# Moving four small copies from ScalarE to VectorE, and a read of PSUM behind a sum, in a fused attention and expert kernel

## The reference

```python
q, k, v = (proj(Wq, bq), proj(Wk, bk), proj(Wv, bv))      # tanh(states @ W + bias), per head
alpha = jnp.einsum('bhqd,bhkd->bhqk', q, k) / jnp.sqrt(jnp.float32(d))
alpha = jnp.where(causal, alpha, jnp.finfo(jnp.float32).min)
alpha = jax.nn.softmax(alpha, axis=-1)
ctx = jnp.einsum('bhqk,bhkd->bhqd', alpha, v)
ctx = ctx.transpose(0, 2, 1, 3).reshape(b, s, h * d)
return jnp.tanh(ctx @ Wo + bo)
...
x = x + _layernorm(_L0_attn_ref(_layernorm(x, axis=-1), ...), axis=-1)
x = x + _layernorm(_L0_ffn_ref(_layernorm(x, axis=-1), ...), axis=-1)
```

## Time and profile before

| | |
|---|---|
| device time of the profiled execution | 1604.17 us |
| its span, first to last instruction | 1602.3 us |
| median of three executions | 1609.84 us |
| TensorE matmul busy | 1522.1 us (95%) |
| VectorE busy | 1394.3 us (87%) |
| ScalarE busy | 1263.1 us (79%) |
| GpSimd busy | 425.2 us (27%) |
| mean granted TensorE clock | 0.990 of full |

### The profile page before, as it was taken

The page is one execution under the profiler, slowest core; times in us unless marked ns, Lnnn a source line. Parts: engine busy times, 40 slices in busy tenths (PEclk is TensorE's granted clock), DMA queues, the critical chain, the costliest instruction groups (busy, mean ns, idle before and its releaser), DMA issues.

```text
span 1602.3 us, 38783 instructions
## 1 busy us (share of the span) xinstructions
PE 1522.1 (95%) x14806; PEld 689.3 (43%) x14806; DVE 1394.3 (87%) x2070; ACT 1263.1 (79%) x1826; POOL 425.2 (27%) x563
## 2 busy tenths in 40 slices
PE   7899999999999999998899999999999999989996
PEld 3344444444444444445233333333333333466774
DVE  6777788888888888898999999999999999397888
ACT  4677777777777777774898999899989999666776
POOL 3311122222122222323235232324332432120004
PEclk9999999999999999999999999999999999899998
DMA  5311001111110011002012000200030000000001
GB/s 149 75 39 41 35 25 41 40 39 39 38 39 29 32 39 40 23 15 54 1 47 50 18 19 19 54 15 15 15 80 15 15 29 2 1 8 8 15 14 53
DMA packets 46606, 52.98 MB, mean 33 GB/s; under 512 B 9279, under 2 KB 33551, under 8 KB 46482
## 3 DMA queue, kind: packets, MB, share of 16 engines
q1 hardware_dynamic: 45584, 50.05, 10.7%
q10 hardware_dynamic: 898, 1.22, 0.3%
HBM read 15.07 MB, written 10.49 MB: 16 GB/s over the span
## 4 chain that ended last, share of the span: by engine, by line
PE 64%; DVE 21%; ACT 10%; issue 3%; POOL 1%; ACTq 0%; POOLq 0%; DVEq 0%
DVE arena L2426 17%; PE psum L592 16%; PE psum L573 12%; ACT arena L2182 7%; PE psum L1934 6%; PE psum L535 5%; PE psum L1565 5%; PE psum L1532 4%; PE psum L630 3%; PE psum L1945 3%; PE psum L609 2%; PE psum L1920 1%; PE psum L555 1%; PE psum L557 1%; PE psum L556 1%
## 5 line engine op out<-in xcount | busy, mean ns | idle before, releaser
L2426 DVE TENSOR_REDUCE arena<-psum 128x2 f32<-128x1024 f32 x490 | 565.5, 1213 | 10.9 <-PE psum L1945 9.6
L2182 ACT ACTIVATE arena<-psum 128x512 f32<-128x512 f32 x980 | 519.6, 601 | 51.6 <-PE psum L1920 45.8
L758 ACT ACTIVATE arena<-psum 128x2048 f32<-128x2048 f32 (+1 forms) x160 | 273.1, 1707 | 127.5 <-PE psum L573 126.0
L1934 PE MATMUL psum<-arena 128*32 128x256 f32 x4096 | 329.2, 393 | 1.4 <-ACT arena L2202 0.2
L592 PE MATMUL psum<-arena,hs 128*64 128x512 f32 (+3 forms) x1536 | 275.9, 494 | 0.0
L1920 PE MATMUL psum<-arena 32*128 32x512 bf16 x1024 | 255.6, 385 | 1.2 <-ACT arena L2182 0.4
L875 POOL TENSOR_SCALAR_AFFINE_SELECT arena<-arena 128x512 f32<-128x512 f32 (+1 forms) x160 | 111.3, 714 | 510.4 <-ACT arena L758 510.4
L573 PE MATMUL psum<-arena 64*128 64x512 f16 (+3 forms) x2304 | 215.8, 325 | 2.1 <-DVE arena L923 1.6
L1945 PE MATMUL psum<-arena 32*128 32x512 bf16 x980 | 189.9, 384 | 20.9 <-DVE arena L2426 13.1
L923 DVE TENSOR_TENSOR arena<-arena 128x1024 f16<-128x1024 f32 x64 | 78.4, 1226 | 102.7 <-ACT arena L737 102.7
L592 PEld LDWEIGHTS psum<-arena,hs 128*64 128x64 f32 x1536 | 96.7, 136 | 157.2 <-issue 149.2
(11 more groups left out here) (223 smaller groups left out, 2038.5 us busy)
## 6 DMA issues: line engine op xcount, KB each, us to landing
arena<-arena SPq DMA_DIRECT2D x30, 512.0 KB, 2.9
arena<-arena SPq DMA_DIRECT2D x46, 128.0 KB, 2.2
arena<-latent_q SPq DMA_DIRECT2D x64, 64.0 KB, 2.0
arena<-latent_k SPq DMA_DIRECT2D x64, 64.0 KB, 2.0
arena<-arena SPq DMA_DIRECT2D x60, 64.0 KB, 2.4
X<-in_L_attn_states SPq DMA_DIRECT2D x4, 512.0 KB, 4.5
latent_q<-arena SPq DMA_DIRECT2D x16, 96.0 KB, 2.3
latent_k<-arena SPq DMA_DIRECT2D x16, 96.0 KB, 2.3
```

Of the source, the lines that this page charges most:

```text
L758: nc.scalar.activation(probs[g], SC[:, :, 0:WIDTH[g]], ACT.Exp, scale=DH ** -0.5).then_inc(exp_done, 1)
L1934: last = nc.tensor.matmul(OT[ROWS * c:ROWS * (c + 1), h * HALF // 2:(h + 1) * HALF // 2], v_cols[par][:, kt, 2 * pr + i, :], e_probs[u % 4 ...
L2182: nc.scalar.activation(e_probs[u % 4][:, i * HALF:(i + 1) * HALF], ring(n, u, i), ACT.Exp, scale=KD ** -0.5).then_inc(e_done, 1)
L2426: nc.vector.tensor_reduce(half_tops[:, kh, qt, 2 * pr:2 * pr + 2], src.rearrange("p (i c) -> p i c", i=2), AX.X, ALU.max).then_inc(top_don ...
```

## The change

`share` moves from ScalarE to VectorE, with the same four copies, the same waits and the same increments. On ScalarE it stood behind the `exp` of group 4; on VectorE it stands directly ahead of `spread`. Besides, in all pairs but the last, `read_denominators` and `invert` now stand behind the second half of `hi_second`, not between the halves. (In pair 31 they stood behind it already.) In the tail, `share(31)` stands ahead of `spread` on VectorE.

```diff
@@ first_scalar @@
-            def share(n):
-
-                act.wait_ge(rden_ready, INVERSE * n + 1)
-                for c in range(4):
-                    half, other = c % 2, c ^ 1
-                    now = slice(half * QB, (half + 1) * QB)
-                    nc.scalar.copy(rden_col[ROWS * other:ROWS * (other + 1), now], rden_col[ROWS * c:ROWS * (c + 1), now]
-                                   ).then_inc(rden_ready, 1)
...
                 exp(i, 4)
-                if at_least(i, 1):
-                    share(i - 1)
...
-            differences_ahead(act, 1, 3)
-            share(N1 - 1)
-            differences_ahead(act, 3, 4)
+            differences_ahead(act, 1, 4)
@@ first_vector @@
+            def share(n):
+
+                dve.wait_ge(rden_ready, INVERSE * n + 1)
+                for c in range(4):
...
+                    nc.vector.tensor_copy(rden_col[ROWS * other:ROWS * (other + 1), now], rden_col[ROWS * c:ROWS * (c + 1), now]
+                                          ).then_inc(rden_ready, 1)
...
                 hi_second(i, par, 0)
-                if at_least(i, 1) and not last:
-                    read_denominators(i - 1)
-                    invert(i - 1)
                 hi_second(i, par, 1)
...
                 if last:
                     first_third_part()
                     first_latent_values()
+                if at_least(i, 1):
                     read_denominators(i - 1)
                     invert(i - 1)
...
                 if at_least(i, 1):
+                    share(i - 1)
                     spread(i - 1)
...
             quads_ahead(dve, 2, 3)
+            share(N1 - 1)
             spread(N1 - 1)
```

More of the change, by code:

```diff
@@ L946, in invert @@
                 nc.vector.reciprocal(rden_col.rearrange("p (h b) -> p h b", h=2), v).then_inc(rden_ready, 1)
+            def share(n):
+                dve.wait_ge(rden_ready, INVERSE * n + 1)
+                for c in range(4):
+                    half, other = c % 2, c ^ 1
+                    now = slice(half * QB, (half + 1) * QB)
+                    nc.vector.tensor_copy(rden_col[ROWS * other:ROWS * (other + 1), now], rden_col[ROWS * c:ROWS * (c + 1), now]
+                                          ).then_inc(rden_ready, 1)
             def spread(n):
```

## The result

The changed kernel takes 1628.42 us (median of 4; 1628.29 to 1636.68), the kernel before, on the same chip, 1608.48 us. The ratio is 1.0141, 95% interval 1.0105 to 1.0177: slower, by about 20 us by the medians and 23 by the ratio. The profiled execution took 1628.19 us, its span is 1625.9 us. All twelve executions of the changed kernel on record lie between 1626.73 and 1639.65 us.

A forecast was written before the change was run, and what follows sets the result against it. TensorE was taken to set the pace in the norm loop's pairs, with whatever delays its starts lost in full. 19.3 + 0.8 + 2.1 + 0.9 = 23.1 us on the median of 1609.84 gave 1633 us, range 1614 to 1642.

The forecast's parts named there:

- The read behind the second half: TensorE's output waits for the late read of PJ: 0.92 us a pair in pairs 10 to 30, 19.3 us.
- by order: Second half of hi_second runs ahead of the read, without meeting GpSimd's mask: output loses 0.59 us a pair.
- the meeting with GpSimd: GpSimd's mask holds the second half until 610.20, raising the pair's loss from 0.59 to 0.92 us.
- Pairs 2 to 9: Moments are missing, so the read costs nothing; copies may spend the 0.04 us cover: 0.1 us a pair, 0.8 together.
- The copies: Four copies on VectorE ahead of spread, 0.20 us each, 0.80 together, hidden by 0.07 us in pair 26.
- the tightest step: In pair 26 the copies fit ahead of ScalarE's rounding by 0.07 us, only because of the stall ahead of them.
- The spill that was a rival: Copies at 0.32 us each or meeting group 0's mask make scale_ctx 0.4 us late: 8 us more, 1641 us; chance 0.13.
- Pair 31: Uncovered copies caught by GpSimd's memsets delay scale_ctx: 2.1 us, or 0 if they slip in first.
- In the tail: Copies stand ahead of the work the last output waits for: 0.9 us, four copies and the overlap lost.
- The sum: 19.3 + 0.8 + 2.1 + 0.9 = 23.1 us on the median 1609.84, giving 1633 us.
- rival of the hidden stall: Small gaps in TensorE's time absorb the late read in the pairs; only 3.8 us remain, 1614 us; chance 0.11.
- rival of a gain on ScalarE: ScalarE paces the pair, so losing 0.88 us of copies shortens 29 pairs: 1588 us; chance 0.06.

The follow-up runs named there:

- third experiment: Kernel with only the read and inverse moved behind the second half, copies on ScalarE; here the tile's two moments also stand behind them. Ratio 1.0006 to the kernel before.
- second kernel: Changed kernel with the read and inverse put back between the halves of hi_second, copies staying on VectorE. Ratio 1.0165 to the kernel before.
- sixth kernels: Copies on VectorE, read between the halves, plus GpSimd's mask of group 0 waiting until the copies are done. Ratio 1.0102 to the kernel before.
- repetition: The whole change run once more, nothing altered, on the chip of the run with the last two copies back on ScalarE. 1629.45 us, ratio 1.0130.
- larger dose: The seventh kernel: copies on ScalarE, read and inverse also behind the first hi_third in pairs 2 to 30. Ratio 1.0498 to the kernel before.

## Why the prediction was right

Right by its direction, and the mechanism by its own steps:

- **The read behind the second half.** Forecast 0.92 us a pair in pairs 10 to 30. Measured 22.33 - 21.41 = 0.92, with 0.85 as the modelled idle. Its two parts were taken apart: 0.59 by order (0.61 measured), 0.33 by the meeting with GpSimd (0.31). The third experiment takes both away at once.
- **Pairs 2 to 9.** Forecast nothing from the read, 0.1 us a pair from the copies. From pair 2 to 9 the change took 149.96 us and the kernel before 149.89: nothing. The copies didn't meet the mask of group 0 there: the third sums, which had waited 0.39 us for the masks of group 3 in pair 5 of the kernel before, don't wait now, and VectorE is that much earlier. It was close: in pair 5 the fourth copy starts 0.01 us ahead of the mask.
- **The copies.** Forecast 0.20 each; 0.196. That they fit by 0.07 us and ahead of the mask was called the tightest step, and it held: the fourth starts 0.10 us ahead of the mask; in the forecast's times they started together. The cover itself was larger than the 0.07 us: `exp` of group 2 still waits 0.17 us for TensorE, since the third sums up to `add_output` took 2.83 us, not 2.91, and ScalarE's rounding came 0.02 us later, not 0.11. The spill that was a rival is what happens as soon as the stall ahead of them shrinks.
- **Pair 31.** Forecast 2.1 us, by the row of L1016; from `output` to the end of `scale_ctx` it is 9.21 against 6.98 us, 2.2. That the size came out is in part luck: the prediction allowed for 2.1 or 0 and took the row; the second and sixth kernels lost 0.7 us in this stretch, by which instruction came first within 0.01 us. In the tail 0.9 was forecast, and the second kernel's trace has 15.87 against 14.96.
- **The sum.** 23.1 us forecast. The traces' own terms give 19.7 (pairs 10 to 30), 0.1, 2.2 and 0.9, together 22.9; the ratio says 23, the medians 20. The times of both kernels scatter by some 8 us, more than the difference between these. The time forecast, 1633 us, is 4.6 us above the median measured.

What the prediction left out is the clock. It counted TensorE's waits as their length alone. In the first trace of the change a stretch at half clock from 77 us on cost 1.6 us, that of pair 31 from the denominators on 1.55, and the tail about 0.8, together 4.0; in the repetition the first and second are missing and the tail lost 2.7. Against that, the profiled execution of before had a half clock of its own from 1382 us on that the changed one didn't have (first row before, second after, beginning at the same work; granted clock third from the end):

```profile
1380.00:1390.00 10.00, 10.00 (x62) 5.31 (x66) 2.43 (x7) 3.30 (x4) 2.13 (x1) 0.59 0.01 2
```

```profile
1407.20:1417.20 10.00, 9.83 (x94) 5.14 (x93) 3.99 (x10) 5.00 (x7) 2.13 (x1) 1.00 0.01 2
```

The same instructions of VectorE come 27.74 us later in the changed kernel ahead of this stretch, and 23.60 behind it: 4.1 us. So the two spans differ by 23.6 us, near the forecast, only because 4.0 us of half clock in the one trace and 4.1 in the other cancel. That is luck of these two traces; the steps rest on the rows of the pairs, not on the spans.

The rival of the hidden stall fell by the larger dose: losses of 0, 0.61, 0.92 and 2.54 us for delays reckoned as 0.06, 0.59, 0.92 and 2.42. The rival of a gain on ScalarE fell too: ScalarE waits 2.75 us for TensorE where its copies stood, the first ScalarE row above.

No kernel tried beats the kernel before. The third equals it: where TensorE shows no wait in a pair, an order of VectorE has no time to give back.

## What to carry to other kernels

Read an order by its distances, not by shares of busy time: for each hand-over, how early the partner is. VectorE was idle for 3.5 us of 21.4, and 0.8 us of copies at one place, or an addition's length ahead of one read, each cost 0.9 to 1.0 us a pair. And the distances belong together: one stall carried the copies past a mask, so undoing it made the kernel slower, and the two halves of the change cost as much alone as together.

## What the runs showed of the hardware

- An addition of two SBUF operands on VectorE that is ready 0.17 us after a mask on GpSimd has begun takes 1.53 us, not 1.22, and GpSimd's next mask is held until it is over. Small one-operand copies are held as well: 0.17 us each alone, 0.50 to 0.63 for the one that meets a mask, and in pair 31, beside a row of memsets, 2.65 for one in two traces, while in two others each passed at the end of one of GpSimd's instructions, after 0.9 us at most. The Trainium skill, page "SBUF — State Buffer", section "Who interferes with whom", has these as an exclusive lock that the first comer keeps for its whole instruction. The traces agree on who waits. They don't quite agree on how long: the held addition ended 0.31 us late, where waiting for the end of the mask of 0.63 us would have made it 0.46. In pairs 28 to 30 it was ready 0.08 us after the mask had begun and took 1.63 us; there too it ended as if it had started 0.15 us ahead of the mask's end.
- The four copies started 0.196 us apart at 0.16 to 0.17 us each, so none overlapped its neighbour, where other VectorE instructions do by 0.08 us. The page "VectorE: DVE Perf Modes", section "Two Vector instructions with no wait between them" of the Trainium skill says that of instructions that start in another group of 32 partitions. The trace agrees.
- After a wait of TensorE of 2.1 to 3.4 us the granted clock fell from 2.4 to 1.2 GHz in some cases and not in others, with the same code before and behind: `output` took 2.74 us or 1.51 behind the same 2.47. In the pairs of the seventh kernel it cost 1.3 to 1.6 us each time. In the trace of the kernel before it fell at 1382 us too, with TensorE busy for the whole of the 20 us ahead of that. What decides it stays open.
